# Attention's small tensor-engine products put side by side: a new order on PE, probabilities transposed by row halves, PSUM banks dealt out anew

## What is computed

```
ln_out = layernorm(hidden_states, ln1_s, ln1_b)
q, k, v = jnp.split(ln_out @ w_qkv + b_qkv, 3, axis=-1)
ctx = merge_heads(attention(split_heads(q), split_heads(k), split_heads(v), ltor_mask))
x = hidden_states + ctx @ w_ao + b_ao
ln_out = layernorm(x, ln2_s, ln2_b)
q = ln_out @ w_q + b_q
k, v = jnp.split(encoder_states @ w_kv + b_kv, 2, axis=-1)
ctx = merge_heads(attention(split_heads(q), split_heads(k), split_heads(v), cross_mask))
x = x + ctx @ w_co + b_co
# then layernorm, gelu MLP, and the recurrent layer

def attention(q, k, v, mask):
    scores = jnp.einsum('bhqd,bhkd->bhqk', q, k) / jnp.sqrt(HD)
    scores = scores * mask - 10000.0 * (1.0 - mask)
    return jnp.einsum('bhqk,bhkd->bhqd', jax.nn.softmax(scores, axis=-1), v)
```

## Time and profile before

| | us |
|---|---|
| median of 3 runs | 1284.46 (1283.63 to 1284.68) |
| the profiled execution | 1283.38 |
| its span, first to last instruction | 1281.6 |
| PE busy in the span | 1173.9 (92%) |
| PE weight loads busy | 987.8 (77%) |
| DVE busy | 982.8 (77%) |
| ACT busy | 759.5 (59%) |
| POOL busy | 601.2 (47%) |

### The profile page before, as it was taken

One profiled execution on the slowest core, in us unless ns is written; L12 is line 12 of the kernel. 1 busy time (PEld: TensorE's weight loads), 2 busy tenths in 40 slices (PEclk: granted clock), 3 DMA queues, 4 the chain that ended last, 5 costly groups with the idle time before them and its releaser, 6 DMA issues. The chain is left out here.

```text
span 1281.6 us, 34708 instructions
## 1 busy us (share of the span) xinstructions
PE 1173.9 (92%) x13056; PEld 987.8 (77%) x13056; DVE 982.8 (77%) x1708; ACT 759.5 (59%) x1681; POOL 601.2 (47%) x520
## 2 busy tenths in 40 slices
PE   5999999999999968999999999999999997854998
PEld 4888889888888857777878877888778775632887
DVE  5777777776666750278999988998988999894787
ACT  4777777777777744455665556655556654333432
POOL 4777777777777730243344334344343343320111
PEclk9999999999999998999999999999999998876999
DMA  9300000011111100000000000000000000000011
GB/s 339 99 2 0 0 0 3 24 40 42 33 41 33 41 3 1 1 1 1 1 1 2 1 1 0 0 0 0 0 0 0 1 1 1 1 1 1 34 41 57
DMA packets 25374, 27.06 MB, mean 21 GB/s; under 512 B 2320, under 2 KB 20048, under 8 KB 24912
## 3 DMA queue, kind: packets, MB, share of 16 engines
q1 hardware_dynamic: 25296, 25.99, 6.0%
HBM read 21.79 MB, written 4.19 MB: 20 GB/s over the span
## 5 line engine op out<-in xcount | busy, mean ns | idle before, releaser
L1370 DVE TENSOR_TENSOR_SCAN late_st<-late_wT,late_st 128x512 f32<-128x512 f32 x128 | 184.5, 1442 | 4.4
L811 POOL TENSOR_TENSOR late_xm<-late_mixed,late_xa 128x512 f32<-128x512 f32 x80 | 93.8, 1182 | 158.1 <-DVE late_mixed L1342 151.8
L273 POOL TENSOR_TENSOR att_z<-att_z,att_row_max 128x512 f32<-128x512 f32 x128 | 131.0, 1046 | 3.5 <-DVE att_row_max L588 0.5
L820 POOL TENSOR_TENSOR late_st<-late_st,late_rT 128x512 f32<-128x512 f32 x32 | 40.7, 1273 | 193.3 <-DVE late_st L1370 193.3
L1364 DVE TENSOR_TENSOR late_st<-psum,late_kT 128x504 f32<-128x504 f32 x128 | 86.7, 677 | 52.6 <-PE psum L996 51.5
L881 PE MATMUL psum<-w,late_hT 128*128 128x256 f32 x512 | 121.7, 382 | 1.9 <-ACT late_hT L1126 1.9
L872 PE MATMUL psum<-late_glnT,w 128*128 128x256 f32 x512 | 120.2, 390 | 2.2 <-ACT late_glnT L1116 2.2
L872 PEld LDWEIGHTS psum<-late_glnT,w 128*128 128x128 f32 x512 | 98.0, 196 | 16.5 <-ACT late_glnT L1116 2.9
L881 PEld LDWEIGHTS psum<-w,late_hT 128*128 128x128 f32 x512 | 94.9, 190 | 19.9 <-issue 5.5
L266 POOL TENSOR_TENSOR att_z<-att_z,cross_bias 128x512 f32<-128x512 f32 x64 | 80.3, 1279 | 58.8 <-DVE att_z L581 57.2
L1126 ACT ACTIVATE late_hT<-psum,cols 128x256 f32<-128x256 f32 x128 | 53.7, 471 | 83.1 <-PE psum L872 83.1
(11 more groups left out here) (167 smaller groups left out, 2828.7 us busy)
## 6 DMA issues: line engine op xcount, KB each, us to landing
att_encT<-in_enc SPq DMA_DIRECT2D x64, 128.0 KB, 2.6
out<-x SPq DMA_DIRECT2D x16, 256.0 KB, 2.0
x<-in_x SPq DMA_DIRECT2D x6, 512.0 KB, 10.3
w<-in_w SPq DMA_DIRECT2D x2, 1024.0 KB, 17.4
cross_mask<-in_cross_mask SPq DMA_DIRECT2D x1, 1024.0 KB, 12.9
w_qkv<-in_w_qkv SPq DMA_DIRECT2D x1, 768.0 KB, 4.5
x<-in_x SPq DMA_DIRECT2D x1, 768.0 KB, 6.0
w_kv<-in_w_kv SPq DMA_DIRECT2D x1, 512.0 KB, 13.7
```

Of the source, the lines that this page charges most:

```text
L273: nc.gpsimd.tensor_tensor(zs, zs, peak.unsqueeze(2).to_broadcast([P, PAIRS, S]), ALU.subtract).then_inc(shifted, 1)
L811: nc.gpsimd.tensor_tensor(xm[:, m % 2, :, :].rearrange("p h (b t) -> p (h b) t", t=S), mixed[:, m % 2, :, :].rearrange("p h (b t) -> p (h ...
L1370: nc.vector.tensor_tensor_scan(states, wT[:, u, half, :, :, :].rearrange("p j b t -> p (j b t)"), states, 0.0, ALU.mult, ALU.add).then_inc ...
```

## The change

PE's body becomes, in one period n: `attend` of n, `transpose_probs` of n+1, `score` of n+3, `transpose_in` of n+5, `transpose_heads` of n, `project_v` of n+4, `project_qk` of n+4, `project_out` of n. The pipeline is one period deeper: periods run from -6 instead of -5.

`transpose_probs` changes its form. Instead of 8 transposes of 128 rows by 128 columns it does 16 of 64 rows by 128 columns: for each pair of heads one for each sequence, that is for each half of the rows. The product is 64 columns wide. The halves go to two banks of their own (6 and 7), and `copy_probs` writes each into its half of every pair's columns. `copy_probs` now waits for all 16 instead of taking each group of four as it comes.

PSUM: banks 0 to 3 as before for scores, with the output projection in bank 0; banks 4 and 5 take the results of `attend` (columns 0 to 255), the transposed input and the transposed heads (bank 4) and the values (bank 5); banks 6 and 7 take the transposed probabilities, and after them the keys (6) and the queries (7). The waits follow: `attend` of n waits for the copies of the values of n+3, of the normalised tile n+4 and of the heads of n-1; `transpose_probs` of n+1 waits for the copies of keys and queries of n+3; `project_qk` of n+4 waits for the copy of the probabilities of n+1. `score` no longer waits for `ln_ready`.

The other engines' bodies are put in another order, one tile further on. ACT: exps, probabilities, normalised tile, heads, values, normalise, queries. DVE: residual, divide, mask, first half of the maxima, keys, second half of the maxima.

```diff
-        proj, tr = core.banks[0], core.banks[1]
-        qh = core.banks[4]
-        out_banks = core.banks[5:7]
-        outs = core.psum[:, 5 * 512:7 * 512].rearrange("p (e n) -> p e n", n=512)[:, :, 0:PAIRS * 32].rearrange(
+        proj = core.banks[0]
+        out_banks = core.banks[4:6]
+        outs = core.psum[:, 4 * 512:6 * 512].rearrange("p (e n) -> p e n", n=512)[:, :, 0:PAIRS * 32].rearrange(
             "p e (r d) -> p e r d", d=32)
-        vv, kk = core.banks[7][:, 0:C], core.banks[7][:, C:2 * C]
+        tr, hh = core.banks[4][:, 0:C], core.banks[4][:, C:2 * C]
+        vv = core.banks[5][:, 0:C]
+        prob_banks = core.banks[6:8]
+        kk, qh = core.banks[6], core.banks[7]
...
-            for n in range(-5, 3):
+            for n in range(-6, 2):
                 body(*divmod(n, TILES), n % 4)
             with eng.Fori(0, (TILES - 12) // 4) as i:
                 for j in range(4):
-                    body(0, 4 * i + (3 + j), (3 + j) % 4)
-            for n in range(TILES - 9, TILES + 3):
+                    body(0, 4 * i + (2 + j), (2 + j) % 4)
+            for n in range(TILES - 10, TILES + 2):
                 body(*divmod(n, TILES), n % 4)
             with eng.Fori(0, (TILES - 8) // 4) as i:
                 for j in range(4):
-                    body(1, 4 * i + (3 + j), (3 + j) % 4)
-            for n in range(ALL - 5, ALL + 1):
+                    body(1, 4 * i + (2 + j), (2 + j) % 4)
+            for n in range(ALL - 6, ALL + 1):
...
+            def attend(k, t, u):
+                n = k * TILES + t
+                pe.wait_ge(probsT_copied, HALVES * (n + 1))
+                pe.wait_ge(v_copied, n + 4 if there(*on(k, t, 3)) else ALL)
+                pe.wait_ge(ln_ready, n + 5 if there(*on(k, t, 4)) else ALL)
+                if later(n):
+                    pe.wait_ge(headsT_copied, n)
+                pe.nop(nofuse=True)
+                for pair in range(PAIRS):
+                    for e in range(2):
+                        keys = slice(e * S, (e + 1) * S)
+                        for b in range(BPT):
+                            rows = slice(b * S, (b + 1) * S)
+                            last = nc.tensor.matmul(out_banks[e ^ b][rows, pair * 32:pair * 32 + HD + 1], zT[keys, pair, rows],
+                                                    values[keys, u, e ^ b, pair, :], start=True, stop=True)
+                last.then_inc(out_ready, 1)
+
+            def transpose_probs(k, t, u):
+                n = k * TILES + t
+                pe.wait_ge(probs_ready, HALVES * (n + 1))
+                pe.wait_ge(k_copied, n + 3 if there(*on(k, t, 2)) else ALL)
+                pe.wait_ge(q_copied, n + 3 if there(*on(k, t, 2)) else ALL)
+                pe.nop(nofuse=True)
+                for pair in range(PAIRS):
+                    for b in range(BPT):
+                        rows = slice(b * S, (b + 1) * S)
+                        last = nc.tensor.transpose(prob_banks[b][:, pair * S:(pair + 1) * S],
+                                                   probs[rows, u % 2, pair, :], core.ident[rows, rows])
+                last.then_inc(probsT_ready, 1)
+
             def score(k, t):
...
-                pe.wait_ge(ln_ready, n + 2 if there(*on(k, t, 1)) else ALL)
...
             def body(k, t, u):
-                if there(*on(k, t, 2)):
-                    score(*on(k, t, 2))
-                if there(k, t):
-                    transpose_probs(k, t, u)
-                if there(*on(k, t, 3)):
-                    project_qk(*on(k, t, 3), u + 3)
-                if there(*on(k, t, 4)):
-                    transpose_in(*on(k, t, 4), u + 4)
                 if there(k, t):
                     attend(k, t, u)
-                if there(*on(k, t, -1)):
-                    project_out(*on(k, t, -1))
+                if there(*on(k, t, 1)):
+                    transpose_probs(*on(k, t, 1), u + 1)
+                if there(*on(k, t, 3)):
+                    score(*on(k, t, 3))
+                if there(*on(k, t, 5)):
+                    transpose_in(*on(k, t, 5), u + 5)
                 if there(k, t):
                     transpose_heads(k, t)
-                if there(*on(k, t, 3)):
-                    project_v(*on(k, t, 3), u + 3)
+                if there(*on(k, t, 4)):
+                    project_v(*on(k, t, 4), u + 4)
+                    project_qk(*on(k, t, 4), u + 4)
+                if there(k, t):
+                    project_out(k, t)
...
-                    act.wait_ge(probsT_ready, HALVES * (n - 1))
+                    act.wait_ge(probsT_ready, n - 1)
...
-                for half in range(HALVES):
-                    act.wait_ge(probsT_ready, HALVES * n + half + 1)
-                    nc.scalar.activation(zT[:, half * 4:(half + 1) * 4, :].rearrange("p r q -> p (r q)"),
-                                         out_banks[half], ACT.Copy).then_inc(probsT_copied, 1)
+                act.wait_ge(probsT_ready, n + 1)
+                for b in range(BPT):
+                    nc.scalar.activation(zT[:, :, b * S:(b + 1) * S], prob_banks[b].rearrange("p (r q) -> p r q", q=S),
+                                         ACT.Copy).then_inc(probsT_copied, 1)
...
             def body(k, t, u):
+                if there(*on(k, t, 2)):
+                    exps(*on(k, t, 2), u + 2)
+                if there(*on(k, t, 1)):
+                    copy_probs(*on(k, t, 1))
+                if there(*on(k, t, 5)):
+                    copy_ln(*on(k, t, 5), u + 5)
                 if there(k, t):
-                    copy_probs(k, t)
-                if there(*on(k, t, 1)):
-                    exps(*on(k, t, 1), u + 1)
-                if there(*on(k, t, 3)):
-                    copy_q(*on(k, t, 3))
+                    copy_heads(k, t)
                 if there(*on(k, t, 4)):
-                    copy_ln(*on(k, t, 4), u + 4)
+                    copy_values(*on(k, t, 4), u % 4)
                 for i in range(2, len(LN_PARTS)):
                     if n_is(k * TILES + t, NORM_AT[i]):
                         invert_deviations(i)
-                if there(*on(k, t, 5)):
-                    normalise(*on(k, t, 5), u + 5)
-                if there(k, t):
-                    copy_heads(k, t)
-                if there(*on(k, t, 3)):
-                    copy_values(*on(k, t, 3), (u + 3) % 4)
+                if there(*on(k, t, 6)):
+                    normalise(*on(k, t, 6), u + 6)
+                if there(*on(k, t, 4)):
+                    copy_q(*on(k, t, 4))
...
                     cross_masks()
-                if there(*on(k, t, 2)):
-                    apply_mask(*on(k, t, 2), u + 2)
-                if there(*on(k, t, 3)):
-                    pad_keys(*on(k, t, 3))
-                if there(*on(k, t, 2)):
-                    find_max(*on(k, t, 2), u + 2, 0)
-                    find_max(*on(k, t, 2), u + 2, 1)
+                if there(*on(k, t, -1)):
+                    add_residual(*on(k, t, -1))
                 if there(k, t):
                     divide(k, t)
-                if there(*on(k, t, -1)):
-                    add_residual(*on(k, t, -1))
+                if there(*on(k, t, 3)):
+                    apply_mask(*on(k, t, 3), u + 3)
+                    find_max(*on(k, t, 3), u + 3, 0)
+                if there(*on(k, t, 4)):
+                    pad_keys(*on(k, t, 4))
+                if there(*on(k, t, 3)):
+                    find_max(*on(k, t, 3), u + 3, 1)
```

`project_qk`, `transpose_in`, `transpose_heads` and `project_v` are moved within the file and keep their products; their waits follow the new banks. Those of `project_qk` are now:

```diff
+            def project_qk(k, t, u):
+                n = k * TILES + t
+                if later(n - 2):
+                    pe.wait_ge(probsT_copied, HALVES * (n - 2))
+                if later(n):
+                    pe.wait_ge(k_copied, n)
+                    pe.wait_ge(q_copied, n)
```

101 lines of the change are left out of this document (37 added, 64 removed).

## The result

The changed kernel takes 1267.6 us (median of 4 runs, 1267.38 to 1269.95) against 1284.56 us in the same comparison: ratio 0.9874, 95% interval 0.9857 to 0.9891. That is faster, clear of the noise, and inside the range of 1246 to 1275, but 12.4 us above the forecast of 1255.2, and outside the 1249 to 1262 that the prediction gave as its own case. The profiled execution took 1267.79 us with a span of 1265.7, which is 15.9 less than 1281.6.

A forecast was written before the change was run, and what follows sets the result against it. PE's own issue was taken as the bound. Self tiles save 35 x 0.47 as (6.90 - 6.43) = 16.4, cross tiles 23 x (7.06 - 6.50) = 12.9, ends nought: 29.3 off 1284.46 gives 1255 us, range 1246 to 1275.

The forecast's parts named there:

- its own case: Whole kernel: the forecast's main case, a time of 1249 to 1262 us, chance 0.54.
- PE's own issue bounds the kernel: Self and cross attention: PE is busy nearly throughout, so only work or switching taken off PE counts.
- Steady tile: Attention: a self tile falls from 6.90 to 6.43 us, a cross tile from 7.06 to 6.50.
- The term for the halves: transpose_probs: two row halves run at once, 0.058 us a pair, 0.46 instead of 0.87, saving 0.41 us a tile.
- its switches and first loads: PE's tile: four changes of form and unhidden first loads, 0.39 + 0.17 = 0.56 to 0.59 us, against 0.67 before.
- the signs named ahead: Profile after: tiles 6.4 to 6.5 us apart, pairs at 0.058, PE busy throughout, DVE, ACT and POOL at 80% or more.
- Putting small products together saves no switches: PE's order: attend, transpose_probs and score use three forms, so four changes of form a period remain, as before.
- the halves save nothing: Rival: a row half can't be loaded while it multiplies, so the 0.41 us is gone; 1279 us, chance 0.10.
- the chains bind: Rival: late exps or division make PE wait at project_qk or transpose_heads every period; 6.70 a tile, 1269 us, chance 0.18.
- What could then wait: Chains from score to copied probabilities and attend to division: slack 0.3 and 0.5 us self; waits 0.02 self, 0.1 cross.
- taken as nought together, each within 3 us: Filling and draining of the attention pipeline: +2.5 us and -2.5 us, nought in sum.
- The start: Filling: score waits about 1 us for the copied queries in each of three periods, +2.5 us.

The follow-up runs named there:

- experiment 6: Kernel before, on DVE only: division moved between the first and second half of the row maxima; 1275.93 us, ratio 0.9939.
- experiment 1: Changed kernel with the probabilities' transposes and their two copies put back to eight of 128x128, new order and banks kept; 1288.28 us, ratio 1.0036.
- experiment 7: Kernel before with two edits: half-row transposes of the probabilities, and on DVE the division between the two maxima; 1269.69 us, ratio 0.9883.
- experiment 2: Kernel before with only the probabilities' transposes changed to 16 by row halves, copies to match, old order of groups; 1285.93 us, ratio 1.0013.
- Experiment 3: Changed kernel with the half-row transposes reordered: all eight of one row half, then all eight of the other; 1288.12 us, ratio 1.0025.
- experiment 5: Changed kernel with DVE's variances and cross masks moved from ahead of the residual to behind the division; 1262.26 us, ratio 0.9831.
- experiment 4: Changed kernel with unread filler transposes on PE in the last three attention periods (4, 6 and 8 in each); 1262.15 us, ratio 0.9836.

## Why the prediction was right, and where it fell short

- **PE's own issue bounds the kernel: right.** The steady tile went down by what came off PE. Where PE idled before (cross tiles), the sum had taken 0.16 of the 7.06 as a wait for the division; experiment 6 took away exactly that, 7.06 to 6.90, and named the ring behind it, which the prediction had not.
- **Steady tile: right.** Forecast 6.43 (self) and 6.50 (cross), measured 6.45 and 6.45. The term for the halves was 0.41, measured 0.38 (experiment 1); a pair of transposes takes 0.063 where the sum had 0.058. One slip is in the sum: its switches and first loads come to 0.56 to 0.59, but 0.59 to 0.61 was added. It is worth 0.02 us a tile. Of the signs named ahead, DVE and ACT stay under their 80% in the self stretch (76 and 79).
- **"Putting small products together saves no switches": right for the order alone,** 6.83 against 6.88. But order and halves are not independent. In the old order the halves pay only 0.19 (experiment 7), and the ring keeps that out of cross tiles (experiment 2). That the other half goes into a fifth change of form, where the new order has four, fits project_qk's 0.11; it is argued from the rows and not tested.
- **Rival "the halves save nothing": wrong as a mechanism.** Experiment 3 measured it. The Trainium skill, "TensorE: Matmul & The Clock Gate", The mechanism, has a weight load overlap a running matmul only where its row group differs. By that rule, as an estimate, the sixteen transposes of experiment 3, which stay in one row group for eight at a time, would have taken some 1.8 us; they took 0.95. The measurement decides against it here. The same section also lets a load run ahead into a background weight buffer, and that is what the trace agrees with.
- **Rival "the chains bind": wrong as stated,** though its number (1269) came closest; it is luck that the range, which takes in this rival, also took in a time that came about another way. PE waits neither for exps nor for the division in steady tiles; cross tiles, where it saw the slack as nil, are at 6.45.
- **What could then wait: the step that failed.** I followed who needs the division and the copied probabilities, and left out who needs the residual. Score starts 1.7 us after project_out's products make way for attend, and both use bank 0, so the residual has to be out within that time. In steady tiles it is. In the four tiles in which DVE does something else first it isn't, and that cost 5.9 us; experiment 5 gave 5.3 back. The sum counted tiles as all alike.
- **Ends "taken as nought together, each within 3 us": the other step that failed.** The drain was to gain 2.5 and lost 3.1, and a further 2.9 was lost behind it, which the sum held to be unchanged. Two things were wrong. I had counted the waits that separate banks save, and not the one of project_out for its own tile's copied heads, which the rows of the drain show. And I had not counted that PE's clock could fall where it rests more: experiment 4 gave 5.5 us back by filling the rests. At full clock the drain is still 0.9 over before and 3.4 over the forecast. A row that could have warned me was in the profile of before: it has half clock for 3.4 us from 37.5 us on, behind a rest of 1.77 us, and for 6.8 from 477.8 on, in a rest of 5.3.
- **The start: the number near (-2.0 against -2.5), partly by luck.** Score waits for the copied queries 0.71 and 0.72 us, two times and not three of 1 us. The rest is a wait of 1.59 for the keys and a gap of 1.86 in the first full period's project_v for which the profile shows no reason; and the start of before was itself 1.5 longer for its half clock.
- **Sum.** 6.4 less in the self stretch, 8.0 less outside the tiles (2.0 + 3.1 + 2.9, against nought), 1.0 more in cross tiles: 13.4 of 29.3 missing, 15.9 saved.

## What to carry to other kernels

A forecast by the steady tile has to be followed by a list of the tiles that aren't steady: every step that an engine does in only a few tiles stands in someone's way once a reorder shortens the time between a product and the reuse of its bank. Put such rare steps behind what PE waits for. And where a pipeline drains into short waits on PE, look at the granted clock there and in the stage behind it: a few useless products were worth as much here (5.5 us) as an edit to the loop (5.3). Before a large reorder, look for a ring through an engine that isn't the bound; here one DVE step put elsewhere took 3.8 us off the cross tiles, and 7.6 in all.

## What the runs showed of the hardware

- In the drain of the changed kernel the granted clock fell to its half level at 439.5 us, in the second of two rests of 1.12 and 1.33 us, and stayed there for 30.7 us, the MLP's first products among them. With the rests filled (experiment 4) it stayed at 1.00 through the drain. Not every such rest does it: after rests of 1.59 and 1.86 us near the start (ahead of 31.3 and 42.3 us) the same kernel kept 1.00.
- Small DVE steps with two inputs in SBUF (128x24 and 128x8, 0.16 to 0.20 us as a rule) took 0.53 to 1.09 us in five places of the changed kernel, and each time ended within 0.1 us behind the end of a POOL step on SBUF. Moved to where POOL was idle or nearly done (experiment 5) they took 0.19 to 0.24. That POOL's step holds them up fits; no run tests it by itself. The Trainium skill, "SBUF — State Buffer", section "SBUF: two separate sides", says that a DVE step with two SBUF inputs and a GpSimd step that reads SBUF exclude each other for a whole instruction. The trace agrees in where the long ones end.
- Half-row transposes within one row half follow each other every 0.063 us, each with a load of 128 columns, against 0.055 for their 64 columns alone, so next to nothing of the load shows. Alternating between the halves brings 16 of them to about 0.5 us.
